# Latents and media brought in turned as well; their means and factors spread through DRAM and applied there by GpSimd

## The reference

```python
xn = layernorm(ctx_1024, gamma_media, beta_media)            # media
ln = layernorm(layernorm(x), gamma_lat, beta_lat)            # latents, normalised twice
q  = ln @ Wq + bq                                            # 8 heads of 128
kv = concat([xn, ln]) @ Wkv + bkv                            # 512 keys
x  = x + tanh(g_xattn) * (softmax(q k^T / sqrt(128)) v @ Wo + bo)
x  = x + tanh(g_ffn) * top2_of_8_experts(layernorm(x))
```

## Time and profile before

| | us |
|---|---|
| three runs, median (lowest to highest) | 1549.94 (1547.97 to 1550.34) |
| profiled execution, its own time | 1549.03 |
| its span, first to last instruction | 1547.3 |
| TensorE busy | 1504.8 (97%) |
| VectorE busy | 1114.0 (72%) |
| ScalarE busy | 950.4 (61%) |
| GpSimd busy | 601.9 (39%) |

### The profile page before, as it was taken

One profiled execution on the slowest core, in us unless ns is written; L12 is line 12 of the kernel. 1 busy time (PEld: TensorE's weight loads), 2 busy tenths in 40 slices (PEclk: granted clock), 3 DMA queues, 4 the chain that ended last, 5 costly groups with the idle time before them and its releaser, 6 DMA issues. The chain is left out here.

```text
span 1547.3 us, 29948 instructions
## 1 busy us (share of the span) xinstructions
PE 1504.8 (97%) x10431; PEld 1385.5 (90%) x10431; DVE 1114.0 (72%) x2689; ACT 950.4 (61%) x2059; POOL 601.9 (39%) x714
## 2 busy tenths in 40 slices
PE   7999999999999999999999999999989999999986
PEld 6889898898888889898898889888989999999986
DVE  6777777777777777777777777777786666666675
ACT  5555656556555555556556555556777777777765
POOL 5323424334342333423334342232454544444433
PEclk9999999999999999999999999999999999999999
DMA  4000101101000000000000000021754545554552
GB/s 152 15 21 8 21 8 21 28 2 28 8 21 8 22 28 8 22 8 22 28 1 28 8 22 8 8 85 66 189 129 127 153 134 128 139 147 128 155 164 56
DMA packets 57823, 91.13 MB, mean 59 GB/s; under 512 B 8521, under 2 KB 44774, under 8 KB 57550
## 3 DMA queue, kind: packets, MB, share of 16 engines
q1 hardware_dynamic: 41710, 70.19, 14.2%
q0 software_dynamic: 15824, 18.98, 6.9%
q10 hardware_dynamic: 144, 0.05, 0.0%
HBM read 70.91 MB, written 18.29 MB: 58 GB/s over the span
## 5 line engine op out<-in xcount | busy, mean ns | idle before, releaser
L887 POOL TENSOR_SCALAR probs<-probs,rsum 128x512 f32<-128x512 f32 x256 | 174.1, 692 | 533.6 <-DVE rsum L1571 531.8
L1100 ACT ACTIVATE pt_hi<-turn 128x512 fp32r<-128x512 f32 x256 | 139.2, 595 | 239.8 <-PE turn L1250 235.7
L912 POOL DMA_INDIRECT out_rows<-yo,token x71 | 122.5, 1725 | 212.5 <-DMA out_rows<-yo,token 149.8
L1688 DVE TENSOR_TENSOR ht_lo<-hs,ht_hi 128x512 fp32r<-128x512 f32 x142 | 98.2, 691 | 121.5 <-ACT ht_hi L1065 115.8
L1565 DVE TENSOR_REDUCE smax<-score 128x1 f32<-128x512 f32 x256 | 169.8, 685 | 11.4 <-PE score L188 10.4
L999 ACT ACTIVATE probs<-score,nbias 128x512 f32<-128x512 f32 x256 | 173.0, 685 | 3.6 <-DVE nbias L1567 3.6
L1056 ACT ACTIVATE hs<-ph,vecs 128x256 f32<-128x256 f32 (+1 forms) x284 | 114.2, 457 | 97.4 <-PE ph L188 88.5
L1798 DVE TENSOR_TENSOR pt_lo<-turn,pt_hi 128x512 fp32r<-128x512 f32 x256 | 164.3, 682 | 10.0 <-ACT pt_hi L1100 9.9
L186 PE MATMUL py<-w_hi,ht_lo 128*128 (+1 forms) x568 | 163.4, 288 | 4.1 <-DVE ht_lo L1688 4.1
L187 PE MATMUL py<-w_lo,ht_hi 128*128 (+1 forms) x568 | 161.0, 284 | 0.0
L188 PE MATMUL py<-w_hi,ht_hi 128*128 (+1 forms) x568 | 161.0, 283 | 0.0
(11 more groups left out here) (251 smaller groups left out, 4711.0 us busy)
## 6 DMA issues: line engine op xcount, KB each, us to landing
w_raw<-in_L_ffn_W SPq DMA_DIRECT2D x45, 1024.0 KB, 17.7
xhat_rows<-rows SPq DMA_DIRECT2D x16, 264.0 KB, 2.2
x_raw<-in_x SPq DMA_DIRECT2D x16, 256.0 KB, 3.6
c_raw<-in_ctx SPq DMA_DIRECT2D x16, 256.0 KB, 3.7
out_rows<-x SPq DMA_DIRECT2D x16, 256.0 KB, 2.8
xg<-xhat_rows,token POOLq DMA_INDIRECT x71, 5.1
out_rows<-yo,token POOLq DMA_INDIRECT x71
v_raw<-in_L_xattn_Wkv SPq DMA_DIRECT2D x2, 512.0 KB, 8.9
```

What stands on the lines that cost most here:

```text
L887: last = pool.tensor_scalar(probs[n % 2][:, t, :], probs[n % 2][:, t, :], rsum[:, n % 2, t:t + 1], 1.0, ALU.mult, ALU.mult)
L912: pool.indirect_dma_start(out=A["out"], out_offset=bass.IndirectOffsetOnAxis(ap=token[:, u:u + 1].bitcast(U32), axis=0), in_=yo_of(t)[:, s ...
L1100: act.activation(pt[0][:, 2 * t:2 * t + 2, :], turn[t][:, :].rearrange("p (j i) -> p j i", j=2), ACT.Copy).then_inc(s_pthi, 1)
```

## The change

Both inputs are also given to the kernel turned, with the 256 rows of a batch along the free dimension (`x_turned`, `ctx_turned`). SP loads a batch of them into `zin` (`load_turned`). GpSimd's `prepare` now only writes the negated means and the factors into `norms`; the four operations that wrote `z` are gone. SP stores `norms` to DRAM as 512 means and 512 factors and loads them back, broadcast to all partitions, into `spread` (`spread_norms`). GpSimd adds the means and multiplies by the factors over `zin` in place (`normalise_turned`, two operations of 128x1024) in step 6, after the probabilities of that step. ScalarE scales `zin` by gamma and beta into `zt` at the end of step 7 (`scale_turned`). The `z` units are out of the plan. `split_kv` stays in step 2 but waits for `zt` alone. For batch 1 these parts stand in steps 2 and 3 of batch 0.

```diff
 A_STEP = 3
+U_STEP = 6
 Z_STEP = 2
...
             units.append(("o", i - 1))
         b, h = i // H, i % H
-        if h == Z_STEP and b + 1 < B:
-            units += [("z", (b + 1, k)) for k in range(KD)]
         if h == T_STEP and 1 <= b < B:
...
+            spread=nc.dram_tensor("mean_and_factor", (B, 2, KEYS), F32, kind="Internal").ap(),
...
             zt = alloc(first, "zt", [P, KD, KEYS])
-            z = alloc(first, "z", [P, JT, D])
+            with ExitStack() as rows_of_first:
+                z = alloc(rows_of_first, "z", [P, JT, D])
+            zin = alloc(first, "z_turned", [P, KD, KEYS])
...
+        norms = sb("norms", [P, 2, JT])
+        with ExitStack() as raws:
+            raw.update(k1=alloc(raws, "k1_raw", [P, KD, INNER - FIRST_W]),
+                       q1=alloc(raws, "q1_raw", [P, KD, INNER - FIRST_W]),
+                       o0=alloc(raws, "o0_raw", [P, H // 2, D]), o1=alloc(raws, "o1_raw", [P, H // 2, D]))
+
+        spread = sb("spread", [P, 2, KEYS])
...
+            def load_turned(c):
+
+                if c == 1:
+                    sp.wait_ge(s_full, KD)
+                else:
+                    sp.wait_ge(s_zt, c - 1)
+                for name, cols in (("x_turned", slice(T, KEYS)), ("ctx_turned", slice(0, T))):
+                    sp.dma_start(zin[:, :, cols], A[name][c].rearrange("(k p) t -> p k t", p=P)).then_inc(s_turned_in, 16)
+
+            def spread_norms(c):
+
+                sp.wait_ge(s_rsa, c)
+                sp.wait_ge(s_z, c + 1)
+                for tiles, cols in ((slice(0, TT), slice(T, KEYS)), (slice(TT, JT), slice(0, T))):
+                    with nc.allow_non_contiguous_dma(reason="a value of each row"):
+                        for r in range(2):
+                            sp.dma_start(dram["spread"][c, r, cols].rearrange("(j p) -> p j", p=P), norms[:, r, tiles])\
+                                .then_inc(s_norms_out, 16)
+                sp.wait_ge(s_norms_out, 64 * c)
+                if c == 1:
+                    weights_split(sp, "k1")
+                else:
+                    sp.wait_ge(s_zin, c - 1)
+                sp.dma_start(spread[:, :, :].rearrange("p r t -> p (r t)"),
+                             dram["spread"][c].rearrange("r t -> (r t)").partition_broadcast(P)).then_inc(s_spread, 16)
...
             sp.wait_ge(s_padz, 1)
             sp.dma_start(dram["xhat"][TOKENS:, :], rows[0][:, 0, :]).then_inc(s_pad, 16)
             sp.dma_start(A["out"][TOKENS:, :], rows[0][:, 0, 0:D]).then_inc(s_pad, 16)
+            load_turned(1)
+            spread_norms(1)
             sp.wait_ge(s_routing, N_ROUTING)
             for r in range(0, LISTS, P):
                 n = min(P, LISTS - r)
                 sp.dma_start(dram["lists"][r:r + n, :], pad_ids[0:n, :]).then_inc(s_pad, 16)
             load(2)
+            load_turned(2)
+            spread_norms(2)
...
+                sp.wait_ge(s_kvt, B)
                 load_w1(0)
-                sp.wait_ge(s_kvt, B)
                 load_w2(0)
...
                 sp.dma_start(ov[b], x2[b % 2][:, :, :]).then_inc(s_x2st[b % 2], 16)
                 if b + 3 < B:
                     load(b + 3)
+                    load_turned(b + 3)
+                    spread_norms(b + 3)
                 sp.wait_ge(s_rows, b + 1)
                 sp.dma_start(rv[b], rows[b % 2][:, :, :]).then_inc(s_rowst[b % 2], 16)
...
                 own.mark(pool.tensor_scalar(ve["a"][:, 0:TT], mv_a[:, 0:TT, 1], 1.0 + EPS, EPS * EPS, ALU.mult, ALU.add))
                 own.mark(pool.tensor_scalar(ve["a"][:, TT:2 * TT], mv_a[:, TT:2 * TT, 1], EPS, 1.0, ALU.add, ALU.mult))
-                pow_rstd("a", rs_a, 4, s_rsa)
-                negate(mv_a)
-                own.wait()
-                pool.wait_ge(s_rsa, c)
-                pool.wait_ge(s_full, number["z", (c - 1, KD - 1)] + 1)
-                for t in range(TT):
-                    norm(z[:, TT + t, :], x_raw[c % 3][:, t, :], mv_a, rs_a, t)
-                for t in range(TT):
-                    last = norm(z[:, t, :], c_raw[c % 2][:, t, :], mv_a, rs_a, TT + t)
-                last.then_inc(s_z, 1)
+                if c >= 2:
+                    pool.wait_ge(s_norms_out, 64 * (c - 1))
+                own.wait()
+                pool.tensor_tensor(norms[:, 1, :], ve["a"][:, 0:JT], minus_half[:, 0:JT], ALU.pow).then_inc(s_rsa, 1)
+                pool.tensor_scalar(norms[:, 0, :], mv_a[:, :, 0], -1.0, 0.0, ALU.mult, ALU.add).then_inc(s_z, 1)
+
+            def normalise_turned(c):
+                pool.wait_ge(s_turned_in, 32 * c)
+                pool.wait_ge(s_spread, 16 * c)
+                means, factors = (spread[:, r:r + 1, :].to_broadcast([P, KD, KEYS]) for r in range(2))
+                own.mark(pool.tensor_tensor(zin[:, :, :], zin[:, :, :], means, ALU.add))
+                own.wait()
+                pool.tensor_tensor(zin[:, :, :], zin[:, :, :], factors, ALU.mult).then_inc(s_zin, 1)
...
             def split_kv(c):
 
-                wait_read(pool, ("z", (c, KD - 1)))
+                pool.wait_ge(s_zt, c)
...
+                if i == 2:
+                    normalise_turned(1)
+                if i == 3:
+                    split_kv(1)
                 if h == A_STEP and b + 2 < B:
                     prepare(b + 2)
-                if h == Z_STEP and b + 1 < B:
+                if h == U_STEP and b + 2 < B:
+                    normalise_turned(b + 2)
+                if h == Z_STEP and 1 <= b < B - 1:
                     split_kv(b + 1)
...
                 act.wait_ge(s_full, n + 1)
-                if kind == "z":
-                    c, k = at
-                    if c:
-                        act.wait_ge(s_kvt, c)
+                act.activation(x2t[:, :, :], src[:, :].rearrange("p (k t) -> p k t", k=KD), ACT.Copy).then_inc(s_aread, 1)
+
+            def scale_turned(c):
+
+                act.wait_ge(s_zin, c)
+                act.wait_ge(s_kvt, c)
+                for k in range(KD):
                     for s in range(2):
-                        last = act.activation(zt[:, k, s * T:(s + 1) * T], src[:, s * T:(s + 1) * T], ACT.Identity,
+                        cols = slice(s * T, (s + 1) * T)
+                        last = act.activation(zt[:, k, cols], zin[:, k, cols], ACT.Identity,
                                               scale=gamma[:, s, k:k + 1], bias=beta[:, s, k:k + 1])
-                else:
-                    last = act.activation(x2t[:, :, :], src[:, :].rearrange("p (k t) -> p k t", k=KD), ACT.Copy)
-                last.then_inc(s_aread, 1)
+                last.then_inc(s_zt, 1)
...
                 for u in steps[i]:
-                    if u[0] in "zt":
+                    if u[0] == "t":
                         read_unit(*u)
+                if i == 2:
+                    scale_turned(1)
+                if i % H == U_STEP + 1 and i // H + 2 < B:
+                    scale_turned(i // H + 2)
...
-                elif kind == "z":
-                    c, k = at
-                    pe.wait_ge(s_z, c + 1)
-                    for j in range(JT):
-                        last = pe.transpose(dst[:, j * P:(j + 1) * P], z[:, j, k * P:(k + 1) * P], ident[:, :])
...
+    for name, of in (("x_turned", "x"), ("ctx_turned", "ctx_1024")):
+        arrays["in_" + name] = np.ascontiguousarray(np.asarray(inputs[of]).transpose(0, 2, 1))
+        aps[name] = nc.dram_tensor("in_" + name, (B, D, T), F32, kind="ExternalInput").ap()
```

More of the change, by code:

```diff
@@ L290, in build @@
             kvt1 = [alloc(first, f"kvt1_{s}", [P, KD, KEYS], F32R) for s in pair]
-            early = dict(zt=zt, z=z, wkv=wkv, wq=wq, kvt=[kvt0, kvt1])
+            early = dict(zt=zt, z=z, zin=zin, wkv=wkv, wq=wq, kvt=[kvt0, kvt1])
             step = dict(v_sb=[[alloc(first, f"v0_{s}", [P, JT, HALF], F32R) for s in pair]])
@@ L355, in late @@
             return sb(name, shape, dt)
-        wkv, wq, kvt, zt, z = (early[n] for n in ("wkv", "wq", "kvt", "zt", "z"))
+        wkv, wq, kvt, zt, z, zin = (early[n] for n in ("wkv", "wq", "kvt", "zt", "z", "zin"))
         raw, v_sb, pt, probs, kt, qt, ot, wo = (
@@ L428, in layer @@
         b1_rows = sb("b1_rows", [P, P])
-        raw.update(k1=sb("k1_raw", [P, KD, INNER - FIRST_W]), q1=sb("q1_raw", [P, KD, INNER - FIRST_W]),
-                   o0=sb("o0_raw", [P, H // 2, D]), o1=sb("o1_raw", [P, H // 2, D]))
+        norms = sb("norms", [P, 2, JT])
[4 more added lines that the diff above has]
+        spread = sb("spread", [P, 2, KEYS])
         x2, rows = [x2_0, x2_1], [rows0, rows1]
@@ L507, in layer @@
         s_z = sem("z_ready")
+        s_turned_in, s_norms_out, s_spread = sem("turned_in"), sem("norms_out"), sem("spread_in")
+        s_zin, s_zt = sem("turned_normalised"), sem("zt_ready")
         s_kvt, s_xn = sem("kvt_ready"), sem("xn_rows")
@@ L1396, in _ @@
                 for u in steps[i]:
-                    if u[0] in "ztgr":
+                    if u[0] in "tgr":
                         unit(*u)
```

## The result

The changed kernel is slower, as forecast: 1618.54 us (1613.55 to 1626.66, 4 runs) against 1548.95 (1546.85 to 1550.34, 4 runs) for the kernel before on the same chip, a ratio of 1.046 (95% interval 1.0419 to 1.0501). The profiled execution took 1613.55 us, its span was 1611.8 and its mean granted clock 0.977; the other three had clocks of 0.964 to 0.969 and spans of 1615.4 to 1624.9.

What follows compares the result with a forecast made beforehand. The prediction took TensorE's own work in the attention stage as the bound. From 1549.0 us: -12.6 z units, +46.8 stops, +19.5 clock, +5.0 start gave 1607.7, say 1608; range 1556 to 1628.

Steps and rivals of the forecast that it cites:

- What bounds the kernel: Attention stage: TensorE's own work, a head step of 7.90 us, with 0.42 us of cover for `kt_lo` in step 7.
- the z units: Step 2 of a batch: removing eight transposes gains 0.90 us in each of fourteen batches, 12.6 us.
- ScalarE, VectorE's step 3, the DMAs: Moved activations, earlier scores and new loads and stores: taken as nothing, at worst 0.1 and 0.3 us a batch for the first two.
- The stops: Step 7, batches 1 to 13: GpSimd's two operations hold VectorE's `weigh`, so TensorE stands 3.6 us each, 46.8 us.
- The clock: After each 3.6 us wait of TensorE the granted clock falls, costing 1.5 us in thirteen batches, 19.5 us.
- The start: Batch 0: ScalarE's `scale_turned` waits for GpSimd's two operations, TensorE is late and its clock falls, together 5.0 us.
- the prediction's own late case: Batch 0: the broadcast lands as late as 9.3 us after its issue near 38, costing 2 us more.
- The rule on VectorE: Small VectorE operations reading and writing SBUF stand until a streaming GpSimd operation ends; those reading PSUM do not.
- the rival of the longer low clock: The clock stays down twice as long after each stop, 13 x 3.4 instead of 13 x 1.5; 1634 us, chance 0.04.
- the other side: GpSimd's new operations leave VectorE alone and the z units' time stays won; 1540 us, 1536 with the start covered, chance 0.15.
- The case of one hold: Only one of GpSimd's two operations holds VectorE's chain, 2.1 us late, 1.5 us a batch; 1559 us, chance 0.14.

Runs made afterwards that it cites:

- e1: The changed kernel with GpSimd's addition and multiplication touching one column of each half instead of 1024; 1537.83 us, ratio 0.9958 to the kernel before.
- e3: The changed kernel with GpSimd's normalising moved to step 0 of the batch before and ScalarE's scaling to step 1, from batch 2 on; 1539.28 us, ratio 0.9984.
- e5: The changed kernel without GpSimd's addition of the means, the multiplication kept; 1570.78 us, ratio 1.0151 to the kernel before.
- r9: The same kernel as e9, run again in a later set; 1539.39 us, ratio 0.9947 to the kernel before.
- e9: e3 with only ScalarE's scaling of batch 1 moved from step 2 to step 3 of batch 0; 1547.61 us, ratio 1.0006 to the kernel before.
- e8: The changed kernel with each of GpSimd's two operations cut into two of 512 columns; 1606.13 us, ratio 1.038 to the kernel before.
- r3: The same kernel as e3, run again in the last set; 1545.12 us, ratio 0.9979 to the kernel before.

## Why the prediction was right, point by point

- **What bounds the kernel** and **the z units**: -12.6 forecast, -12.5 found in the steps, and e1 and e3 show it as a gain when nothing takes it back. The rows decided rightly: the 275 ns for each transpose of the Trainium skill ("TensorE: Matmul & The Clock Gate", Part 4) would have made it 31, as an estimate.
- **ScalarE, VectorE's step 3, the DMAs: nothing.** Held: e1 has all of them, and its batches are 65.6 us. The norms' stores were mispriced, but in the steady part 22 us of slack hide it.
- **The stops.** Mechanism as forecast (two holds, the reciprocal between them, the maximum 4.2 us late forecast and 3.99 found). The wait is 3.1 to 3.3 us instead of 3.6, yet in the two batches that kept their clock (7 and 9) step 7 grew by 11.49 - 7.97 = 3.52, some 0.3 more than the wait itself. 13 x 3.52 = 45.8 against 46.8.
- **The clock.** What is left of the stops is 68.8 - 45.8 = 23 us, 1.8 each, where 1.5 was taken; by the batch it is from 0 to about 2.6. That each wait would bring the fall was wrong for batches 7 and 9. The other three executions have lower clocks and longer spans, as more or longer falls would give, but they weren't profiled.
- **The start: mis-sized**, 5.0 forecast, 7.9 found. The step that failed is the landing: the prediction took 2.1 us for the stores of `norms`, from a gather of 4-byte values in the earlier trace rows, and so had the broadcast issued near 38. SP went on from the stores only 9.1 us after the last issue, and issued it at 43.04. The broadcast of 512 KB took only 3.9, less than the 9.3 taken at the worst, so the two errors partly cancelled: GpSimd's addition began 2.0 us later than forecast (46.96 against 44.97), near the prediction's own late case. The maximum of step 3 came at 55.49 instead of 53.4, and the rest, 0.8 us, is what TensorE lost behind it.
- **Not foreseen**: the longer step 2 of batches 3 and 7, +5.0 here, 4.2 of it behind ScalarE's wait. The earlier trace rows show none, since the profiled execution of the kernel before had hardly any: only step 2 of batch 4 was 0.3 us longer than the others.
- **The rule on VectorE was too wide.** That "a small VectorE operation that reads and writes SBUF stands" holds for the kinds in rows 3 and 4 and in `weigh`, but BATCH_NORM_AGGREGATE does both and ran free under the same stream (64 times at most 0.185 us). The forecast wasn't touched by it, since the two operations of `weigh` that it had held are a TENSOR_SCALAR and a TENSOR_TENSOR.
- **Two sums at the edges.** The upper end of the range, 1628, is 3 us more than 13 stops of 6.4 us give (1549.0 - 12.6 + 83.2 + 5.0 = 1624.6), and the rival of the longer low clock comes to 1632.4 and not to 1634. Neither moves a chance.
- **The rivals.** Of the four, the other side (VectorE left alone) is what e1 and e3 look like in their steady batches. Their times of 1537.83 and 1539.28 lie in the 1536 to 1540 worked out only because their chip was a faster one (1545.09 for the kernel before): by the ratios, 0.9958 and 0.9984, they won 7 and 3 us, where 9 to 13 was worked out, and batch 0 has the difference. It needed the stream to be gone or elsewhere. The case of one hold is e5: 1570.78 measured, 1559 worked out; its own profiled time of 1566.73 is 1549.0 - 12.5 + 13 x 1.5 + 5.5 for its batch 0 (75.18) = 1561.5, and one-off stops in batches 3, 7 and 9 (3.2 + 0.7, 2.5 and 1.3), less 2.6 at the ends.

The sum of 1607.7 is 5.8 us short of the profiled execution's 1613.55: 2.9 of the start, 5.0 of one-off stops and 2.5 of the stops with their clock are missing in it, and 4.8 at the two ends of the kernel came back. That the last two unforeseen parts nearly cancel, +5.0 and -4.8, is luck. The median of the four executions, 1618.54, is 10 us above the forecast of the median (1607.7 + 0.9), and 1626.66, the slowest, is barely inside the range; the profiled one had the highest clock of the four.

## What to carry to other kernels

Before work is moved onto GpSimd, look at what small TENSOR_SCALAR and TENSOR_TENSOR operations between SBUF tiles VectorE runs at that hour, not at GpSimd's idle share: here a chain of them was held once for each GpSimd stream it met, and cutting each stream in two didn't free it (1.038 against 1.046). The same two operations cost 68.8 us in step 6 and nothing two steps later, where VectorE is reading PSUM; of the versions run, r9, with that place and the later scaling at the start, is the fastest with the whole computation, 0.5% faster than before on its chip, though the same program was no faster in e9. A round trip through DRAM in single values took 13 to 15 us from the first issue to the landing, and the start of this kernel had no slack for it.

## What the runs showed of the hardware that was not expected

- Stores of single 4-byte values (4 x 1 KB) held SP long. In the steady part too, far from the busy start, in the changed kernel:

```profile
984.41 1.90 SPq L726 DMA_DIRECT2D mean_and_factor<-norms  x4
993.57 0.33 SPq L733 DMA_DIRECT2D spread<-mean_and_factor  x1
```

  From the end of the issues, 986.31, to SP's next one it is 7.3 us, 9.1 at the start and 8.0 in the mean of the fifteen (120.1 / 15). The gather of such values in the other direction landed in 2.1.
- Waits of TensorE of 3.1 to 3.3 us brought the lower clock in eleven batches and not in two (the windows above), and one of 3.20 in e9 did not either; waits of 1.1 to 1.2 us (e5) never did. What decides between equal waits stays open.
- ScalarE stood 2.5 to 5.6 us before one `ot_hi` (in e8 4.8 before a `v_hi`) in step 2 of some batch, in the kernel before as in the changed one, and TensorE lost up to 6 us by it. The cause wasn't found.
- The stretch from batch 15 on, in the main the stage of the experts, varied by up to 12.8 us from profile to profile. e3 and r3 are one program: their spans differ by 5.9 us, and 5.2 of it lies there, so ScalarE's waits are not the whole of the spread of 1541.2 to 1554.06 over ten runs of the unchanged kernel. What varies there stays open.
- BATCH_NORM_AGGREGATE from SBUF to SBUF was not held by the GpSimd stream that held TENSOR_SCALAR, 28 times out of 28.
